# Two adjacency products with normalisation: column 1 of the tiles moved from row pairs ahead of time to seven-product sets in its own rows, and the first tile sum made earlier

## What is computed

```python
x_drop = x * (u >= 0.1) / 0.9
h   = layernorm(x + adj @ x_drop)                 # first product with adj (8192 x 8192)
out = layernorm(h + adj @ (h @ weight) + bias)    # second product with the same adj
```

## Time and profile before

| | |
|---|---|
| median of three runs | 910.28 us |
| the profiled execution, device time | 910.34 us |
| its span, first to last instruction | 908.6 us |
| TensorE busy | 877.6 us (97%) |
| VectorE busy | 540.9 us (60%) |
| HBM read | 356.61 MB, 395 GB/s over the span |
| mean granted TensorE clock | 0.991 |

### The profile page before, as it was taken

One profiled execution on the slowest core, in us unless ns is written; L12 is line 12 of the kernel. 1 busy time (PEld: TensorE's weight loads), 2 busy tenths in 40 slices (PEclk: granted clock), 3 DMA queues, 4 the chain that ended last, 5 costly groups with the idle time before them and its releaser, 6 DMA issues.

```text
span 908.6 us, 13717 instructions
## 1 busy us (share of the span) xinstructions
PE 877.6 (97%) x5754; PEld 410.9 (45%) x5754; DVE 540.9 (60%) x1043; ACT 30.4 (3%) x75; POOL 25.1 (3%) x24
## 2 busy tenths in 40 slices
PE   4799999999999999999999999999999999999996
PEld 3554233333343444535354554636446456356342
DVE  6466222116044756756676676868667768768556
ACT  0000000000000000000000000000000000000011
POOL 3000000000000000000000000000000000000123
PEclk9899999999999999999999999999999999999998
DMA  9999999999999999999999999989899999999952
GB/s 327 411 417 419 420 419 422 422 420 414 419 420 420 420 421 420 421 393 413 420 419 393 406 399 395 421 337 421 360 403 420 410 409 419 415 421 419 422 215 70
DMA packets 59085, 359.61 MB, mean 396 GB/s; under 512 B 6544, under 2 KB 14736, under 8 KB 16784
## 3 DMA queue, kind: packets, MB, share of 16 engines
q1 hardware_dynamic: 59024, 358.74, 96.3%
HBM read 356.61 MB, written 2.10 MB: 395 GB/s over the span
## 4 chain that ended last, share of the span: by engine, by line
PE 90%; DMA 4%; DVE 2%; SPq 1%; issue 1%; ACT 0%; DVEq 0%
PE psum L971 22%; PE psum L924 21%; PE psum L906 8%; PE psum L939 8%; PE psum L933 7%; PE psum L957 6%; PE psum L892 4%; PE psum L913 4%; PE psum L977 4%; DMA tiles<-adj_chunks 3%; PE psum L869 2%; DMA tiles<-adj 1%; PE psum L992 1%; PE psum L1007 1%; SPq L481 1%
## 5 line engine op out<-in xcount | busy, mean ns | idle before, releaser
L650 DVE TENSOR_TENSOR layer<-psum,layer 128x512 f32<-128x512 f32 (+1 forms) x143 | 98.6, 690 | 202.0 <-PE psum L971 102.9
L924 PE MATMUL psum<-tiles,stat 128*64 128x512 f32 x976 | 216.9, 593 | 0.8 <-DMA tiles<-adj_t 0.8
L971 PE MATMUL psum<-tiles,stat 128*64 128x512 f32 x944 | 211.7, 594 | 0.0
L924 PEld LDWEIGHTS psum<-tiles,stat 128*64 128x64 f32 x976 | 71.0, 137 | 128.2 <-issue 120.4
L971 PEld LDWEIGHTS psum<-tiles,stat 128*64 128x64 f32 x944 | 66.7, 137 | 123.5 <-issue 121.2
L941 PE MATMUL psum<-tiles,stat 128*64 128x256 f32 x360 | 92.7, 380 | 0.0
L906 PE MATMUL psum<-tiles,stat 128*64 128x256 f32 x360 | 92.4, 379 | 0.0
L908 PE MATMUL psum<-tiles,stat 128*64 128x256 f32 x360 | 92.4, 379 | 0.0
L682 DVE TENSOR_TENSOR tiles<-tiles 128x512 f32<-128x512 f32 x90 | 62.3, 692 | 40.3 <-PE psum L915 38.1
L906 PEld LDWEIGHTS psum<-tiles,stat 128*64 128x64 f32 x360 | 49.3, 137 | 40.9 <-issue 20.0
L685 DVE TENSOR_TENSOR tiles<-tiles 128x512 f32<-128x512 f32 x90 | 62.3, 692 | 3.1
(11 more groups left out here) (94 smaller groups left out, 858.6 us busy)
## 6 DMA issues: line engine op xcount, KB each, us to landing
tiles<-adj_t SPq DMA_DIRECT2D x306, 1024.0 KB, 13.0
tiles<-adj SPq DMA_DIRECT2D x12, 1024.0 KB, 18.9
tiles<-adj_chunks SPq DMA_DIRECT2D x12, 1024.0 KB, 20.9
tiles<-adj_parts SPq DMA_DIRECT2D x16, 256.0 KB, 14.5
x_res<-x SPq DMA_DIRECT2D x16, 128.0 KB, 13.4
out<-layer SPq DMA_DIRECT2D x8, 256.0 KB, 2.1
tiles<-u SPq DMA_DIRECT2D x3, 512.0 KB, 10.4
tiles<-x SPq DMA_DIRECT2D x3, 512.0 KB, 11.2
```

Of the source, the lines that this page charges most:

```text
L650: return dve.tensor_tensor(out=to, in0=addend, in1=to, op=ALU.add)
L924: last = pe.matmul(sum_f[i % 2][to, :], stat[:, j * C + c, 0:D], tile[:, c], start=begun.get("f") != i and c < 2, stop=ends and c >= 2, sk ...
L971: last = pe.matmul(bank[to, :], stat[:, j * C + c, D:2 * D], tile[:, c], start=c == 0, stop=c == C - 1)
```

## The change

- Column 1 leaves the early jobs (EARLY_COLUMNS = 1). In rows 2 to 15 the tile (i, 1) becomes a raw/fused set of its own row: 104 sets, where the code before makes 90 (the words of the change say 91). Row 2 gets its first set, and with it a combine.
- The sums of x and h are made for block 1 too. They live in one home more of `stat_homes`.
- The first of a set's four sums becomes an instruction group of its own, `first_sums`. It is issued up to three tile jobs before the end of the raw job, but not before the tile's slot has been freed for its load, and not before the turn or row end that precedes the raw job. It still waits for the tile to land.

```diff
 EARLY = 2
-HOMES = (NB - 2 - EARLY) // 2
+EARLY_COLUMNS = 1
+HOMES = (NB - 2 - EARLY) // 2 + 1
+AHEAD = 3
 def begins_at(i):
-    return EARLY if i >= EARLY else 0
+    return EARLY_COLUMNS if i >= EARLY else 0
 def has_fused(i):
-    return i > EARLY
+    return i >= EARLY and i > begins_at(i)
 ...
-        if 1 <= i - 1 < EARLY:
+        if 1 <= i - 1 < EARLY_COLUMNS:
             early = sorted(early + [("early", r, i - 1) for r in range(EARLY, NB, 2)], key=lambda job: job[1:])
 ...
+    latest_freed, freed_for = 0, {}
+    for load in loads:
+        latest_freed = max(latest_freed, load[3])
+        freed_for[load[0], load[5]] = latest_freed
+    first_sums_from, second_sums_from, chain_at = [], [], 0
+    for job in jobs:
+        if job[0] in ("row_end", "turn"):
+            chain_at = done_after[job]
+        elif job[0] == "fused":
+            raw_done = done_after["raw", *job[1:]]
+            first_sums_from.append(min(raw_done, max(raw_done - AHEAD, freed_for[job[1:3], "raw"], chain_at)))
+            second_sums_from.append(raw_done)
 ...
-            home = layer1_pair(j) if j % 2 else stat_homes[:, (j - EARLY) // 2]
+            home = layer1_pair(j) if j % 2 and j > EARLY else stat_homes[:, j // 2]
 ...
+            def first_sums(n):
+                slot, load = place[fused_jobs[n], fused_jobs[n][1:3]]
+                tile, right = tiles[:, slot], slice(B // 2, B)
+                dve.wait_ge(s_arrived[slot], 16 * load)
+                dve.tensor_tensor(out=tile[:, 0:2, right], in0=tile[:, 0:2, right], in1=tile[:, 2:4, right],
+                                  op=ALU.add).then_inc(first_sums_ready, 1)
 ...
-                slot, load = place[fused_jobs[n], (i, j)]
-                dve.wait_ge(s_arrived[slot], 16 * load)
-                dve.tensor_tensor(out=tile[:, top, right], in0=tile[:, top, right], in1=tile[:, bottom, right],
-                                  op=ALU.add).then_inc(first_sums_ready, 1)
                 dve.wait_ge(first_sums_ready, n + 1)
 ...
-                    while n_second_sums < len(fused_jobs) and second_sums_from[n_second_sums] <= n_tile_jobs:
-                        second_sums(n_second_sums)
-                        n_second_sums += 1
+                    while n_second_sums < len(fused_jobs):
+                        if n_second_sums < n_first_sums and second_sums_from[n_second_sums] <= n_tile_jobs:
+                            second_sums(n_second_sums)
+                            n_second_sums += 1
+                        elif n_first_sums < len(fused_jobs) and first_sums_from[n_first_sums] <= n_tile_jobs:
+                            first_sums(n_first_sums)
+                            n_first_sums += 1
+                        else:
+                            break
 ...
-                    if EARLY <= job[1] < NB - 2:
+                    if EARLY_COLUMNS <= job[1] < NB - 2:
                         sum_stat(job[1])
```

More of the change, by code:

```diff
@@ L308, in resnorm_graph_layers @@
     tile_jobs = [job for job in jobs if job[0] in TILE_JOBS]
-    second_sums_from = [done_after["raw", *job[1:]] for job in fused_jobs]
+    latest_freed, freed_for = 0, {}
[10 more added lines that the diff above has]
+            second_sums_from.append(raw_done)
     joined = []
@@ L652, in _ @@
             n_tile_jobs = 0
-            n_second_sums = 0
+            n_first_sums = n_second_sums = 0
             n_combined = 0
@@ L830, in stat_sums_of @@
                 nonlocal stat_sums_seen
-                if j - EARLY + 1 > stat_sums_seen:
-                    pe.wait_ge(stat_sums_ready, j - EARLY + 1)
-                    stat_sums_seen = j - EARLY + 1
+                if j - EARLY_COLUMNS + 1 > stat_sums_seen:
+                    pe.wait_ge(stat_sums_ready, j - EARLY_COLUMNS + 1)
+                    stat_sums_seen = j - EARLY_COLUMNS + 1
             def h_of(turned_rows):
```

## The result

The changed kernel takes 912.33 us, the median of eleven runs (911.64 to 912.57), against 910.30 us before (eleven runs, 909.51 to 911.14): ratio 1.0022, 95% interval 1.0013 to 1.0031. The forecast was 912.4 us.

The account below looks back on a forecast made before the run. In rows 2 to 5 TensorE and the loads were both taken to run at their limit. -5.7 + 10.9 - 3.1 = +2.1 us on 910.34 us gave 912.4 us, range 909.6 to 915.5 us.

Parts of the forecast that it names:

- Part 1: TensorE's work, rows 2 to 15: seven early jobs out (48.0 us), 14 sets in (42.3 us), -5.7 us without new waits.
- Part 2: Rows 2 to 5: tile (5, 14) lands at 262.8 us; TensorE waits 10.9 us for loads up to there.
- the form that was named: Rows 2 to 5: some 10 us of TensorE waits for tiles, in pieces under 0.8 us at `first` jobs.
- Part 3: Consecutive fused jobs, as in row 9: the first sum ahead shortens TensorE's waits for VectorE, -3.1 us in all.
- What costs nothing: Rows 2 to 15: VectorE's 56 more sums and 28 fewer joins, +19 us, lie beside matmuls and add no time.
- the loads keep up: Rows 2 to 5: loads don't hold TensorE up, its gain arrives: 901.5 us, up to 908; chance 0.10.
- the waits are shorter: Rows 2 to 5: loads at 2.49 us, up to 4.0 us gained on sums: 909.5 to 910.4 us; chance 0.22.
- the first sum blocks VectorE's queue: Rows 2 to 6: it waits for late tiles, up to 2.5 us per place: 914 to 917 us; chance 0.12.
- over 3 us for landing behind the pairs: Before most raw jobs, pairs leave over 3 us for the tile to land, so the sum ahead wouldn't block VectorE.
- The clock rival: Rows 2 to 4: with TensorE idling, its clock falls to 1.2 GHz, adding 18 us, some 930 us; chance 0.05.

Follow-up runs that it names:

- the half loads: Changed kernel, but only two of four chunks loaded for the 27 tiles of rows 2 to 4 used once, matmuls all made: 900.36 us.
- the half alone: Kernel before, column 1 still in seven early jobs, with only the first sum issued up to three jobs ahead: 906.79 us, ratio 0.9966.
- Half the work: Changed kernel, but 25 `first` jobs of rows 2 and 3 make two of their four products, loads unchanged: 912.15 us.

## Why the prediction was right

**Part 1**, -5.7 us of TensorE's work, stands. TensorE's matmul count rose from 5754 to 5922 as 14 sets of 28 replaced 7 jobs of 32, and where the loads don't matter (the half loads) the time is 900.36 us, against 901.5 us computed with the parts 1 and 3.

**Part 2**, the landing of (5, 14) at 262.8 us, stands: 262.9 measured. Two errors cancel in it. The place that (2, 6) had in the queue is now that of (2, 1), whose load is issued at 109.6 and lands 26.0 us later, at 135.6 and not at 136.4: the x load of row 2 stands behind it now, and the execution was 0.4 us earlier at the turn of row 1, from the loads at the very start. The 50 loads from there, with four x loads among them, took 127.3 us, 2.55 us each and not 2.53. So TensorE alone would have been at (5, 14) at 251.5 and waited 11.4 us, not 10.9. The waits have the form that was named, fourteen pieces at `first` jobs, of which two (0.91 and 1.00 us) exceed the 0.8 us that was named. From (5, 14) to the last job before the turn of row 15 the changed kernel takes 29.8 us longer, eleven sets less the gain of part 3.

**Part 3** was low by a few tenths. I gave each place 0.15 us that remains, and -3.1 us in all. Two fused jobs now take 3.54 us against 3.44, so 0.1 us remains in each of six places: 5 x 0.7 less 0.1 for the new place is -3.4 us, and the half alone gained 3.3 us. What the sum left out is that the columns would have made these waits longer and one more, 1.3 us, had the first sum stayed; as both parts came together, it had no effect on the total.

**What costs nothing** holds, with a wrong count in it. An early job has two joins of VectorE and not four: line 650 stands 143 times in the page before, its counterpart, line 664, 129 times after. So 14 joins went and not 28, and VectorE's busy time rose by 27.0 us. As no matmul waits for VectorE's sums or joins behind row 1, the sum stays as it was.

**The rivals.** That the loads keep up falls by the timeline, and by the halved bytes. That the waits are shorter falls too, since they came to 11.4 us. That the first sum blocks VectorE's queue doesn't happen at three jobs: the first sum does wait there for tiles, four times and 20.0 us together, but no matmul waits for a sum. At eight jobs the mechanism is real. One place cost 2.4 us of waits, within the 2.5 that I gave it, and 1.7 us more because the clock fell behind them, which I had only as a rival of its own; all places together cost 13.6 us. The reason given against it, over 3 us for landing behind the pairs, holds for three jobs and not for eight. The clock rival falls too: the granted clock is 1.00 in the window of rows 2 to 5. Half the work, with longer pauses, did lower it, and so did one pause of the run with eight jobs ahead, as the last section shows.

The forecast was right by its own steps, and their errors are small: the landing 0.1 us late, the stretch behind it 29.8 us longer instead of 33.2 - 3.1 = 30.1. That the landing is so close is luck in part, as two errors of 0.8 us cancel there. That the median came within 0.1 us of 912.4 is closer than the steps can claim, since the runs of the changed kernel alone spread over 0.9 us.

## What to carry to other kernels

An engine that is 97% busy and a queue that is full in the same stretch have to be accounted separately: up to the last job that finds its data just landed, time is a number of loads, and only behind it is it work. Jobs with more work per byte are what keeps the engine going in a stretch of light jobs, so making them cheaper, or moving them out of it, gives back less than it removes, or more than all of it. A step that is issued ahead in a queue in order should go just far enough to use an idle gap; farther, it waits for data with everything else behind it.

## What the runs showed of the hardware

I had not expected the clock to answer to short pauses. In the run with half the work TensorE was idle for 1.4 of every 2.5 us in rows 2 and 3 while at full clock, never longer at a time, and the granted clock fell. Two of its windows (columns as above):

```profile
165.00:176.00 11.00, 8.22 (x24) 1.73 (x23) 0.68 (x1) 0.59 (x1) 0.00 (x0) 0.69 1.02 419
176.00:188.00 12.00, 6.59 (x24) 1.42 (x24) 4.44 (x14) 0.62 (x2) 0.00 (x0) 0.84 1.01 421
```

In the timeline of that run above, the four matmuls of a job take 1.08 us up to 182.03 and 1.98 us from 184.52 on, the two levels of 2.4 and 1.2 GHz. In the changed kernel, with 0.56 us idle in every 2.49 us, the clock stayed at 1.00. The prediction drew on the Trainium skill, TensorE: Matmul & The Clock Gate, section "Why this matters for your kernels", for pauses: that one long pause loses the full clock and short ones don't. For the pauses of 0.56 us this trace agrees; the pauses of 1.4 us lost it, so there the measurement decides against the rule as that section has it. It cost no time here, since the slower jobs (the four matmuls of one at 184.52 to the next job at 187.01) still fitted between two loads.

In the run with eight jobs ahead it did cost time. There TensorE had one pause of 1.86 us, at 237.30, and a short one behind it; then the clock was at 0.50 from 239.0 to 242.4, and its matmuls started 0.42 us apart and not 0.21. At 454.35 in the same run it had a pause of 1.20 us, and the clock stayed at 1.00. Which property of the pauses decides isn't shown by these runs.
